# The dense layer behind attention in two sets of eight row tiles: seven block products of four banks each, twice

## What is computed

```python
x = x + attention(layernorm(x), ctx_4096, ctx_4096, ...)     # Wo at its end: stages before the change
W = scales_full * (w - zeros_full)                            # 1024 x 1024, unpacked from 4 bits
x = x + (layernorm(x).reshape(-1, 1024) @ W + bias)           # 2048 rows, all in float32
```

## Time and profile before

| | |
|---|---|
| runs | median 2234.64 us of 3 (2229.41 to 2236.3) |
| the profiled execution | 2235.26 us, its span 2233.5 us |
| TensorE in the span | 98% busy |
| granted TensorE clock, mean | 0.995 |
| busy over the span: DVE, POOL, ACT | 64%, 67%, 49% |

### The profile page before, as it was taken

The page is one execution under the profiler, slowest core; times in us unless marked ns, Lnnn a source line. Parts: engine busy times, 40 slices in busy tenths (PEclk is TensorE's granted clock), DMA queues, the critical chain, the costliest instruction groups (busy, mean ns, idle before and its releaser), DMA issues.

```text
span 2233.5 us, 33060 instructions
## 1 busy us (share of the span) xinstructions
PE 2196.9 (98%) x10358; PEld 1838.8 (82%) x10358; DVE 1436.9 (64%) x2575; ACT 1094.6 (49%) x2339; POOL 1493.0 (67%) x1048
## 2 busy tenths in 40 slices
PE   9999999999999999999999999899999999999799
PEld 7888888888888888788888888788888888888587
DVE  4772574777777778877777777523555354755867
ACT  3132123767667667767666766632233333433322
POOL 2320553788888889888888888665665464564475
PEclk9999999999999999999999999999999999999899
DMA  7766675687888888887787887698665555484644
GB/s 267 262 227 219 241 265 197 206 253 240 250 252 241 241 253 270 257 254 243 240 253 236 246 260 230 202 318 276 223 229 192 183 193 169 153 292 157 201 148 174
DMA packets 320844, 514.46 MB, mean 230 GB/s; under 512 B 25440, under 2 KB 205952, under 8 KB 320256
## 3 DMA queue, kind: packets, MB, share of 16 engines
q1 hardware_dynamic: 305312, 476.30, 67.7%
q10 hardware_dynamic: 14688, 35.13, 4.0%
q0 software_dynamic: 768, 2.10, 0.3%
HBM read 325.72 MB, written 187.71 MB: 230 GB/s over the span
## 4 chain that ended last, share of the span: by engine, by line
PE 83%; DVE 8%; POOL 4%; issue 2%; DMA 2%; ACT 1%; SPq 0%; ACTq 0%; DVEq 0%; POOLq 0%
PE ps L264 18%; PE ps L265 18%; PE ps L266 18%; PE ps L945 8%; PE ps L947 8%; PE ps L946 8%; PE ps L976 1%; PE ps L978 1%; PE ps L977 1%; POOL s_buf L1803 1%; DVE turned L1662 1%; DVE rope_tmp L1340 1%; ACT wq_t L1007 1%; POOL rope_tmp L1803 1%; DVE rope_tmp L1339 1%
## 5 line engine op out<-in xcount | busy, mean ns | idle before, releaser
L264 PE MATMUL ps<-act_t,wq_t 128*128 128x512 f32 x1280 | 500.4, 391 | 1.8 <-DVE wq_t L1329 0.9
L265 PE MATMUL ps<-act_t,wq_t 128*128 128x512 f32 x1280 | 499.6, 390 | 0.0
L266 PE MATMUL ps<-act_t,wq_t 128*128 128x512 f32 x1280 | 498.0, 389 | 0.0
L1881 POOL TENSOR_TENSOR b_parts<-wraw,b_parts 128x512 fp32r<-128x512 f32 x140 | 241.1, 1722 | 283.9 <-ACT b_parts L1166 227.6
L945 PE MATMUL ps<-b_parts,a_parts 128*128 128x512 f32 x896 | 349.0, 390 | 2.1 <-issue 1.1
L947 PE MATMUL ps<-b_parts,a_parts 128*128 128x512 f32 x896 | 348.6, 389 | 0.0
L946 PE MATMUL ps<-b_parts,a_parts 128*128 128x512 f32 x896 | 348.6, 389 | 0.0
L1516 DVE TENSOR_TENSOR a_parts<-xring,a_parts 128x1024 fp32r<-128x1024 f32 x112 | 145.7, 1301 | 306.7 <-ACT a_parts L1161 306.7
L1862 POOL TENSOR_TENSOR q_t<-pt_raw,q_t 128x1024 fp32r<-128x1024 f32 x124 | 302.7, 2442 | 45.0 <-ACT q_t L1144 42.1
L1803 POOL TENSOR_TENSOR rope_tmp<-rope_tmp 128x512 f32<-128x512 f32 x144 | 193.5, 1344 | 182.2 <-DVE rope_tmp L1340 182.2
L1161 ACT ACTIVATE a_parts<-xring 128x1024 fp32r<-128x1024 f32 x112 | 118.8, 1061 | 394.0 <-PE ps L947 383.6
(11 more groups left out here) (165 smaller groups left out, 4474.0 us busy)
## 6 DMA issues: line engine op xcount, KB each, us to landing
sq_scratch<-scores SPq DMA_DIRECT2D x124, 512.0 KB, 3.0
pt_raw<-sq_scratch SPq DMA_DIRECT2D x496, 128.0 KB, 4.0
xring<-left_scratch SPq DMA_DIRECT2D x112, 512.0 KB, 3.8
left_scratch<-s_buf SPq DMA_DIRECT2D x64, 640.0 KB, 5.1
wraw<-in_L_xattn_Wq SPq DMA_DIRECT2D x64, 512.0 KB
wraw<-in_L_xattn_Wo SPq DMA_DIRECT2D x64, 512.0 KB, 4.5
v_scratch<-kv_t ACTq DMA_DIRECT2D x32, 512.0 KB, 3.6
k_scratch<-kv_t ACTq DMA_DIRECT2D x32, 512.0 KB, 3.9
```

The source lines that it names most:

```text
L264: eng.matmul(dst, lh, rh, start=(k == first), stop=False)
L265: eng.matmul(dst, lh, rl, start=False, stop=False)
L266: mm = eng.matmul(dst, ll, rh, start=False, stop=(k == last))
L1881: pool.tensor_tensor(b_parts[:, s % 2, 1, :], src, b_parts[:, s % 2, 0, :].bitcast(F32), ALU.subtract).then_inc(right_lo, 1)
```

## The change

The rows are taken in two sets: set g = 0 is row tiles 0 to 7, set g = 1 is 8 to 15, and the 2 x 2 scheme is applied inside each set (its row halves are tiles 0 to 3 and 4 to 7 of the set). A product now has four row tiles, so four banks, and a step 4 x 3 = 12 matmuls. There are 2 x 7 x 4 = 56 steps. Each right operand is loaded and split in both sets. D_M1, D_M2, D_M7 and D_M4 use banks 0 to 3, D_M6, D_M5 and D_M3 banks 4 to 7. The parts have three slots instead of two (a left part is now 128x512), so ACT waits for step s - 3. All sums of left blocks are made by DVE, two steps ahead, from blocks that stay in SBUF; those of D_M6 in set 0 in the last four steps of the Wo stage. `add_second` is one a step in D_M7, D_M4, D_M5. The layer norm of rows 8 to 15 is spread: `product_out` over x = 0, 1, statistics over x = 2 to 5, `row_scaled` one a step at x = 6 to 13, `turn_row` one a step at x = 7 to 14, stores at x = 15 to 22, loads at x = 22 to 29. For these rows ACT reads the row with a stride of eight elements and writes it dense, and DVE transposes a dense row, where before ACT read and wrote dense and DVE read with the stride of eight.

```diff
-        END = STEPS + 7 * KS
+        SET = 7 * KS
+        END = STEPS + 2 * SET
         def dense_part(s):
-            return (s - STEPS) // KS, (s - STEPS) % KS
+            return (s - STEPS) // SET, (s - STEPS) % SET // KS, (s - STEPS) % KS
+        def part_a(s):
+            j = (s - STEPS) % 3
+            return a_flat[:, j * E:(j + 1) * E].rearrange("p (l c) -> p l c", l=2)
+        def part_b(s):
+            j = (s - STEPS) % 3
+            return b_parts[:, j, :, :] if j < 2 else a_flat[:, 3 * E:4 * E].rearrange("p (l c) -> p l c", l=2)
+        def bank_of(d, i):
+            return i + (4 if d in (D_M6, D_M5, D_M3) else 0)
...
             for s in range(STEPS, END):
+                g, d, k = dense_part(s)
+                x = s - STEPS
                 if s + 3 < END:
                     dense_right(s + 3)
+                if 15 <= x < 23:
+                    if x == 15:
+                        sp.wait_ge(y_turned, 16)
+                    j, a0 = (x - 15) // 2, (x - 15) % 2 * 2
+                    for a in (a0, a0 + 1):
                         store_turned(sp, 1, 2 * j, 2 * j + 2, a, turned_stored[j])
+                if 22 <= x < 26:
+                    sp.wait_ge(turned_stored[x - 22], 8 * 16)
+                    sp.wait_ge(left_summed, sum_count(0, D_M5, x - 22))
+                    sp.dma_start(left_c[:, x - 22, :], turned_block(1, 2 * (x - 22))).then_inc(side_in[x - 22], 16)
...
+            for i in range(4):
+                store_out(1, D_M3, i)
...
             def dense_step(s):
+                g, d, k = dense_part(s)
...
+                for i in range(4):
                     if k == 0:
+                        if d == D_M2:
+                            pe.wait_ge(d_copied, 4 * g + i + 1)
+                        elif g == 0 and d in (D_M1, D_M6):
+                            pe.wait_ge(m_out, 48 + bank_of(d, i) + 1)
...
                         else:
+                            pe.wait_ge(d_out, out_count(g, {D_M7: D_M2, D_M4: D_M7, D_M5: D_M6, D_M3: D_M5}[d], i))
...
             def row_scaled(dst, r):
-                act.activation(dst, rows[:, r, :], ACT.Identity, bias=ln_tmp[:, 3, r:r + 1],
+                src = rows[:, r, :]
+                if r >= 8:
+                    dst, src = dst.rearrange("p (k c) -> p k c", k=KT), src.rearrange("p (c k) -> p k c", k=KT)
+                act.activation(dst, src, ACT.Identity, bias=ln_tmp[:, 3, r:r + 1],
...
             def dense_hi(s):
-                act.wait_ge(step_done, s - 1)
+                act.wait_ge(step_done, (STEPS - 1, STEPS, STEPS)[s - STEPS] if s < STEPS + 3 else s - 2)
...
+            def dense_sum(g, d, k):
+                if d == D_M6:
+                    dve.tensor_tensor(sum_view(second[k]), y_half(left_c, k, 1), y_half(left_b, k, 1), ALU.add)
+                    dve.tensor_tensor(sum_view(second[k]), sum_view(second[k]), y_half(left_c, k, 0), ALU.subtract)
+                elif d == D_M7:
+                    dve.tensor_tensor(sum_view(third[k]), y_half(left_c, k, 0), y_half(left_c, k, 1), ALU.subtract)
+                elif d == D_M5:
+                    dve.tensor_tensor(sum_view(third[k]), y_half(left_c, k, 1), y_half(left_b, k, 1), ALU.add)
+                elif d == D_M3:
+                    dve.tensor_tensor(sum_view(second[k]), y_half(left_b, k, 0), sum_view(second[k]), ALU.subtract)
...
...
             for s in range(STEPS, END):
+                g, d, k = dense_part(s)
+                x = s - STEPS
                 dense_lo(s)
-                if s + 1 < END:
-                    dense_sum(s + 1)
+                if s + 2 < END and s + 2 >= STEPS + 2 * KS + KS:
+                    dense_sum(*dense_part(s + 2))
+                if x < 2:
+                    product_out(M6, range(4 * x, 4 * x + 4))
+                for r in ((), (), (8, 9, 10), (11, 12, 13), (14, 15))[x] if x < 5 else ():
+                    half_stats(r, 1)
+                if x == 5:
+                    inverse_std(2, 8, 8)
+                    mean_scaled(8, 8)
+                if 7 <= x < 15:
+                    turn_row(xn[:, r % 4, :], r)
+                if k == 1 and s >= STEPS + 2 * KS and d != D_M2:
+                    dense_out(g if d > D_M1 else g - 1, d - 1 if d > D_M1 else D_M3)
...
+            def add_second(g, d, i):
+                dst = rows[:, 8 * g + i + (0 if d == D_M5 else 4), :]
+                pool.wait_ge(d_out, out_count(g, D_M6, i))
+                dst = dst[:, 0:NW] if d == D_M4 else dst[:, NW:E]
+                pool.tensor_tensor(dst, dst, spare[:, 4 * g + i, :], ALU.add).then_inc(u_added, 1)
             for s in range(STEPS, END):
                 step_lo(s)
+                if x in (7, 9, 28, 30):
+                    add_bias(r)
+                if d in (D_M7, D_M4, D_M5):
+                    add_second(g, d, k)
```

More of the change, by code:

```diff
@@ L333, in dense_left, with bank_ready @@
             if d == D_M1:
[L334 to L339, removed]
+                return y_half(left_c, k, 0)
+            if d in (D_M2, D_M4):
+                return y_half(left_b, k, 0 if d == D_M2 else 1)
+            return sum_view(second[k] if d in (D_M6, D_M3) else third[k])
+        def bank_ready(eng, g, d, i):
+            if i < 3:
+                eng.wait_ge(m_done, 49 + 3 * (7 * g + d) + i + 1)
             else:
-                eng.wait_ge(step_done, STEPS + (d + 1) * KS)
+                eng.wait_ge(step_done, dense_step_of(g, d, KS - 1) + 1)
         def store_turned(eng, tset, k0, k1, a, done):
@@ L674, in _ @@
                     sp.dma_start(left_c[:, k, :], turned_block(0, 2 * k)).then_inc(side_in[k], 16)
+                if 104 <= s < 108:
+                    k = s - 104
+                    sp.dma_start(left_b[:, k, :], turned_block(0, 2 * k + 1)).then_inc(main_in[k], 16)
             def dense_right(s):
-                d, k = dense_part(s)
+                _, d, k = dense_part(s)
                 sp.wait_ge(right_lo, s - 1 if s < STEPS + 2 else s - 3)
                 sp.dma_start(right_slot(s), w_dram[k, :, D_RIGHT[d], :]).then_inc(right_loaded(s)[0], 16)
[L681 to L698, removed]
             def store_half(r, n):
@@ new lines, in _ @@
+                if k >= 2:
+                    for i in (2 * k - 4, 2 * k - 3):
+                        if d == D_M6:
+                            store_out(g, D_M2, i)
+                        elif d == D_M5:
+                            store_out(g, D_M4, i)
+                        elif d == D_M3:
+                            store_out(g, D_M5, i)
+                        elif d == D_M1 and g == 1:
+                            store_out(0, D_M3, i)
+            for i in range(4):
+                store_out(1, D_M3, i)
@@ new lines, in dense_out @@
+            def dense_out(g, d):
+                for i in range(4):
+                    bank_ready(dve, g, d, i)
+                    low, high = rows[:, 8 * g + i, :], rows[:, 8 * g + 4 + i, :]
+                    if d == D_M6:
+                        dve.wait_ge(d_copied, 4 * g + i + 1)
+                        dst = spare[:, 4 * g + i, :]
+                    elif d == D_M2:
+                        dve.wait_ge(biased, 6 * g + i + 1)
+                        dst = low[:, 0:NW]
+                    else:
+                        if d == D_M5:
+                            dve.wait_ge(d_out, out_count(g, D_M7, i))
+                        dve.wait_ge(u_added, added_count(g, {D_M7: D_M7, D_M4: D_M4, D_M5: D_M7, D_M3: D_M5}[d], i))
+                        dst = low[:, NW:E] if d == D_M3 else high[:, 0:NW] if d == D_M4 else high[:, NW:E]
+                    dve.tensor_tensor(dst, ps[:, bank_of(d, i), :], dst, ALU.add).then_inc(d_out, 1)
@@ L1736, in dense_out @@
[L1736 to L1757 removed]
+                hi, lo = [part_a(s)[:, l, :].rearrange("p (r a i) -> p a r i", r=4, a=4) for l in range(2)]
```

261 lines of the change are left out of this document (93 added, 168 removed).

## The result

The changed kernel takes 2251.92 us (median of four runs, 2248.26 to 2253.47) where the kernel before takes 2233.9. The ratio is 1.0078, its 95% interval 1.0065 to 1.0091: slower, by 18.0 us between the medians (0.78% is 17.4 us). The forecast was 2233.2, the range 2219 to 2246. The profiled execution took 2248.26 us (span 2246.5), the lowest of the four.

A forecast was written before the change was run, and what follows sets the result against it. PE was taken to bound the kernel, losing 25.2 us in the last stage, mostly to the layer norm of rows 8 to 15. New losses summed to 23.8 us, so -1.4 us: 2233.2 us, range 2219 to 2246.

The forecast's parts named there:

- start: x = 0 to 6: parts late at x = 1, 2 and 6, 0.8 us in all, bounds 0 and 3.
- ACT's stride: ACT's strided scaling of rows 8 to 15: between 1.23 and 2.1 us each, taken a fourth of the way, 1 us lost.
- entry to D_M7: Set 0, x = 13: POOL's split queued behind an addition awaiting DVE's first D_M6 result; loss 3.0 to 7.0, taken 5.9 us.
- POOL's rounds: D_M7 to D_M3: rounds of 3.02 us, 3.5 with a DVE sum, in 2.72 us steps; loss 6.8 + 6.3 us.
- bank wait of D_M3: D_M3 reuses D_M5's banks, which DVE empties late: 0.8 us a set.
- double sums: Set 1's D_M6: double sums fill DVE, three operations a step and a queue of results, 1 us.
- entry in set 1: Entry to D_M7 in set 1, DVE free: 3.1 us needed against 2.72, loss 0.4 us.
- Banks: DVE reaches D_M5's results behind D_M3's second step's split and sum, 0.8 us a set, 1.6; D_M4 0.4, covered.
- a full wait of DVE too: Upper bound on POOL's rounds: DVE also waiting in full in D_M5 would add 3 us a set.
- two strides and a full DVE: Slower rival: ACT's stride at x = 7 to 14 4 us, DVE full in D_M5 5, entry 1.5; 2243 us, chance 0.18.
- The clock: Slower rival: short PE idles in 24 steps bring 1.2 GHz, 43 us more, 2276 us, chance 0.05.
- POOL keeps up: Faster rival: DVE's operations fall into POOL's idle moments, eleven rounds cost nothing, 16 us won, 2218 us, chance 0.20.

The follow-up runs named there:

- no_adds: The changed kernel without POOL's 24 additions of the shared product and the waits for them (that part of the result left out): 2231.64 against 2233.87 us before, ratio 0.9989.
- outs_first: The changed kernel with DVE taking D_M5's four results right behind the left split of D_M3's first step: 2239.65 against 2233.87 us before, ratio 1.0027.
- outs_all: The changed kernel with the results of D_M6, D_M7 and D_M5 right behind the split in the next product's first step: 2238.63 against 2235.3 us before, 1.0016.
- outs_adds: outs_all with each POOL addition one step later, behind the next step's right split: 2236.51 against 2235.3 us before, ratio 1.0004.
- m7_early: ordered, with DVE's left sums for D_M7 at x = 6 to 9 and 30 to 33 and biases moved: 2234.47 against 2234.33 us before, 1.0009.
- ordered: outs_adds with bias additions moved, DVE's to x = 26, 27, 32, 33, POOL's to 25, 27: 2235.16 against 2235.3 us before, ratio 1.0000.
- spread: ordered with ACT's scaling and DVE's transposes in two steps of three, stores and loads later: 2237.3 against 2235.3 us before, ratio 1.0008.

## Why the prediction was wrong

Its sum and what the changed kernel's trace shows, both as us lost in the stage (a step's start to the next, less 2.72, so that a wait counts with the step before it; half rate apart, as what the steps right behind a long wait take over 2.72):

| part | predicted | measured |
|---|---|---|
| x = 0 to 11 (start, ACT's stride) | 0.8 + 1 | 5.6 |
| entry to D_M7, set 0 (x = 13) | 5.9 | 5.0 |
| POOL's rounds, set 0 | 6.8 | 1.8 |
| bank wait of D_M3, set 0 | 0.8 | 5.3 |
| x = 25 to 40 and the wait at x = 41 (double sums, biases, entry in set 1) | 1 + 0.4 | 5.2 |
| POOL's rounds, set 1 | 6.3 | 4.6 |
| bank wait of D_M3, set 1 | 0.8 | 5.2 |
| matmuls at half rate behind these waits | 0 | 8.5 |
| sum | 23.8 | 41.1 |

For instance 2127.48 to 2135.51 is 8.03 us, less 2.72 gives 5.3; the half rate is 2.9 us at x = 13 and 14, 1.7 at x = 24, 1.4 at x = 30, 2.4 at x = 52. (The first line of the prediction's sum, 177.7 less 152.3, is 25.4; with 0.23 for the last matmul, as in the 41.1, it is its 25.2.)

**The step that failed is the one called Banks.** It had the place and the mechanism right (DVE reaches D_M5's results behind the split and sum of the second step), but priced it at 0.8 us a set, where it is 5.3 and 5.2, and 4.1 more at half rate. The prediction had let DVE's operations of 512 elements cost POOL 0.5 us and taken DVE itself at 0.6 each; "a full wait of DVE too" stood only as a bound of 3 us. In fact both wait: 1.7 us each, in turns. Six such operations of DVE in a row (2123.95 to 2134.09, three sums and three splits) are 10.1 us in place of 3.6, so DVE is 6.5 us later when it comes to the results than it would be alone. no_adds shows the price, outs_first that the order makes it a wait of PE: 12.3 us by moving four instructions a set. A better use of the rows of before was at hand: in the earlier trace rows DVE's operation beside POOL went from 1.22 to 2.20 us, which is 1.0 a time, and D_M5 has two such operations in every step.

**The half rate** had no term at all, although show it behind the waits of 3.77 and 4.36 us, and the sum itself forecast a wait of that length (5.9 us at x = 13). It is half of the 17 us by which the sum was short. How much of it falls on one execution is partly chance, as x = 30 in outs_all and outs_adds shows. The prediction's reading that a wait of 2.85 us leaves the full rate and only longer ones bring the half rate didn't hold even in its own trace. In the kernel before PE also waits at x = 5:

```profile
2090.55 0.68 PE L976 MATMUL ps<-b_parts,a_parts 128*128 128x512 f32 x1 [2.24 <-DVE a_parts L1718]
```

and the eight matmuls from there on start 0.43 us apart or more.

**POOL's rounds** were sized right as rounds (3.02 forecast, 2.95 measured in m7_early; 3.5 forecast with a sum, 3.4 measured) and wrong as a loss: the prediction worked out that a part is ready 3.1 us early and then charged every round in full. A lead is spent before PE feels anything; with 3.1 us of it in each set 13.1 becomes 6.9, measured 6.4. That the two agree is partly luck: by set it would be 3.7 and 3.2, and 1.8 and 4.6 were measured; why the sets differ wasn't tried. This error went the other way and hid part of the first two.

**x = 0 to 11.** ACT's strided scaling was taken at a fourth of the way, 1 us in all; it takes 2.35 us, the upper end and more, so ACT's step is 3.3 us (two splits of 0.52 and the row's 2.25) against 2.72, and PE waits 0.36 to 1.19 us at each of x = 6, 7, 8 and 10. The Trainium skill (SBUF — State Buffer, section Door 1: The DMA port swizzle, its note on cachelines) was the better guide: its rule doesn't ask which engine reads, and ACT's 2351 ns for 1233 agree with it. The steps x = 1 to 4 also took 2.8 to 3.0 us without a wait that the profile names; what that is was not tried. **The biases** of x = 28 to 31 had no term; DVE does one of 2.3 us ahead of its split, and PE waits 3.06 us at x = 30:

```profile
2152.77 2.27 DVE L1682 TENSOR_TENSOR rows<-rows,bias_rows 128x1024 f32<-128x1024 f32 x1
2154.97 1.74 DVE L1777 TENSOR_TENSOR a_parts<-left_c,a_parts 128x512 fp32r<-128x512 f32 x1
```

(in the changed kernel, DVE in order of time).

**What was right.** The wait at x = 13 is for POOL and is the longest but for D_M3's, 5.0 for 5.9 us; no wait for `turned` or `left_b` remains; the transposes and the stores cost nothing visible; the 28 more boundaries cost nothing (x = 32 to 36 start 2.72 apart). Of the rivals, *two strides and a full DVE* came nearest with 2243; with the 8.5 us of half rate added it would have been at the time measured, partly by luck. Its 4 us for ACT came (5.6 where 1.8 stood in the sum), its 1.5 for the entry did not, and for its 5 in D_M5 the waits at D_M3 took 8.9 over the sum, while POOL's rounds took 6.7 less. *The clock* didn't come as it was put, by short idle moments: from x = 40 to 50 PE was busy 32.19 of 35.25 us, with waits of 0.2 to 0.7 us ahead of seven of the steps x = 41 to 51, and the granted clock stayed 1.00. The half rate came behind single waits of 3 to 5 us. *POOL keeps up* was true for most of the rounds and won little.

## What to carry to other kernels

When work moves to an engine that must be on time, write out its program in order from the last moment when it was idle to the instruction that others wait for, and price each operation as it runs beside its neighbour, not alone: here 1.7 for 0.6 us, six times in a row. Put the emptying of a buffer that another engine waits for ahead of the preparation that has a lead; moving four instructions in each of two sets was worth 12 us. A lead between engines is a stock, to be taken from the loss once. And a long wait can bring the half rate and then costs the matmuls behind it on top.

The best order found equals the kernel before and doesn't beat it: the stage of ordered is 178.5 us long and loses 26.2 us, where the one before lost 25.2, only in other places. In the changed kernel POOL is busy for 131.7 us of the stage instead of 101.6 and DVE for 158.3 instead of 136.7, the turns included, and both are full in D_M5; whether the kernel would gain with some of this work on another engine wasn't tried.

## What the runs showed of the hardware

- A DVE operation of 128x512 between two SBUF operands takes 0.68 us alone and 1.78 beside a POOL that is always busy; POOL's goes from 1.30 to 1.75. In such a stretch a round of one DVE and one POOL operation takes 1.70 us. DVE's additions from PSUM (2.47 for four, with a POOL operation of 1.30 beside them, at 2120.96 in the changed kernel) and its transposes (1.23) keep their time beside POOL's work.
- ACT pays for a read of float32 at a stride of 32 bytes as DVE does: 2351 ns for 1233, and DVE 2149 for 1231, for 128x1024.
- After a wait of 2 us or more the number of matmuls at half rate is not the same from run to run: at x = 13 seven behind 2.03 us in ordered, none behind 2.49 in spread; at x = 30 none behind 3.08 in outs_all, fourteen behind 3.08 in outs_adds; thirteen behind 4.72 in the changed kernel. It makes such a wait cost 0 to 3 us more than its length.
- The work ahead of the stage, the same in all of these kernels but for its last steps, ended within 7.5 us of one another in the profiles (the stage began at 2048.0 to 2055.5), so only the length of the stage can be compared between single profiles, and the whole only by medians.
